# A four-layer graph network on one core: one-hot work split over two stages, 512 rows of zeros, deeper lags

## The reference

```python
h = jnp.maximum(_layernorm(x, axis=-1), 0.0)
x = x + _L0_gnn_ref(h, src, dst, edge_weight, ...)     # sum over edges into src of w * (h @ W)[dst], + bias
h = jnp.maximum(_layernorm(x, axis=-1), 0.0)
x = x + _L1_gnn_ref(h, edge_index, ...)                # attention: softmax over the edges into dst
h = jnp.maximum(_layernorm(x, axis=-1), 0.0)
x = x + _L2_gnn_ref(h, edge_index, ...)                # hypergraph: sum into dst, scale, sum back into src
h = jnp.maximum(_layernorm(x, axis=-1), 0.0)
x = x + _L3_gnn_ref(h, ..., src, dst, edge_attr_4, edge_attr_8, ...)  # tensor product, sum into dst
```

## Time and profile before

| | us |
|---|---|
| median of 3 runs (lowest to highest) | 3779.65 (3775.08 to 3782.87) |
| the profiled execution | 3784.34 |
| its span in the trace | 3782.5 |
| POOL busy (share of the span) | 2403.0 (64%) |
| DVE busy | 2003.5 (53%) |
| PE busy | 1933.2 (51%) |
| ACT busy | 920.8 (24%) |
| mean DMA rate | 115 GB/s |

### The profile page before, as it was taken

One profiled execution on the slowest core, in us unless ns is written; L12 is line 12 of the kernel. 1 busy time (PEld: TensorE's weight loads), 2 busy tenths in 40 slices (PEclk: granted clock), 3 DMA queues, 4 the chain that ended last, 5 costly groups with the idle time before them and its releaser, 6 DMA issues.

```text
span 3782.5 us, 39731 instructions
## 1 busy us (share of the span) xinstructions
PE 1933.2 (51%) x8526; PEld 1456.1 (38%) x8526; DVE 2003.5 (53%) x6412; ACT 920.8 (24%) x2412; POOL 2403.0 (64%) x2088
## 2 busy tenths in 40 slices
PE   0000037777668689889363233666666466664000
PEld 0000025555644367777253222443333365563000
DVE  6964325555999655554786555222222299995000
ACT  0000024443000144544133444222222222221000
POOL 0767777788880477775003564788888754448887
PEclk9999987777999755555576555555555578886555
DMA  2999623355650132332377998666666544445443
GB/s 82 297 298 333 209 59 87 84 66 68 97 66 0 33 80 78 78 80 66 94 230 134 114 124 121 138 120 130 119 124 126 115 144 145 140 143 96 37 36 34
DMA packets 449411, 437.32 MB, mean 116 GB/s; under 512 B 77855, under 2 KB 359493, under 8 KB 449027
## 3 DMA queue, kind: packets, MB, share of 16 engines
q0 software_dynamic: 128576, 119.75, 26.0%
q1 hardware_dynamic: 280262, 283.65, 23.8%
q10 hardware_dynamic: 40512, 33.32, 3.6%
HBM read 262.12 MB, written 174.41 MB: 115 GB/s over the span
## 4 chain that ended last, share of the span: by engine, by line
POOL 21%; DVE 9%; issue 8%; DMA 7%; PE 2%; ACT 2%; DVEq 1%; SPq 0%; ACTq 0%; POOLq 0%
POOL out_dram L654 15%; POOL work L640 5%; DVE work L1668 3%; DMA he<-work 3%; DMA work<-flags_clip 1%; DMA work<-gat_h 1%; DVE big L1998 1%; DVE work L1654 1%; DVE work L1963 1%; DVE work L1966 1%; PE bank L829 1%; ACT work L1175 1%; DVE work L1644 0%; DMA out_dram<-big,idx_add_d 0%; PE bank L954 0%
## 5 line engine op out<-in xcount | busy, mean ns | idle before, releaser
L1668 DVE TENSOR_TENSOR_SCAN work<-work,bank 128x512 f32<-128x512 f32 (+1 forms) x343 | 426.5, 1265 | 462.4 <-PE bank L829 220.4
L640 POOL DMA_INDIRECT work<-d,idx_run_d x196 | 189.6, 967 | 379.0 <-DVEq L286 264.6
L829 PE MATMUL bank<-ident,work 128*128 128x128 f32 x588 | 151.3, 407 | 456.1 <-ACT work L1175 238.6
L1175 ACT ACTIVATE work<-work 128x128 f32<-128x128 f32 x784 | 317.4, 481 | 257.8 <-DVE work L1663 244.0
L654 POOL DMA_INDIRECT out_dram<-work,idx_add_s x196 | 311.4, 1589 | 60.2 <-issue 59.1
L654 POOL DMA_INDIRECT out_dram<-big,idx_add_s x196 | 308.8, 1575 | 62.6 <-issue 53.7
L654 POOL DMA_INDIRECT out_dram<-big,idx_add_d x196 | 306.7, 1565 | 59.7 <-issue 55.2
L640 POOL DMA_INDIRECT work<-s,idx_e_d x196 | 203.4, 1038 | 209.9 <-DVE work L1963 160.0
L707 POOL DMA_INDIRECT big<-out_dram,idx_src_d x196 | 195.6, 998 | 200.7 <-DVEq L286 141.2
L829 PEld LDWEIGHTS bank<-ident,work 128*128 128x128 f32 x588 | 98.5, 204 | 508.3 <-ACT work L1175 176.8
L640 POOL DMA_INDIRECT work<-rec_d,idx_e_s x196 | 218.0, 1112 | 77.7 <-issue 58.2
(11 more groups left out here) (324 smaller groups left out, 5283.2 us busy)
## 6 DMA issues: line engine op xcount, KB each, us to landing
out_dram<-big SPq DMA_DIRECT2D x71, 726.0 KB, 8.2
big<-in_x_dram SPq DMA_DIRECT2D x71, 704.0 KB, 7.0
work<-flags_src SPq DMA_DIRECT2D x98, 256.0 KB, 3.8
work<-flags_dst SPq DMA_DIRECT2D x98, 256.0 KB, 3.7
edge_w<-work SPq DMA_DIRECT2D x49, 512.0 KB, 3.7
work<-edge_w ACTq DMA_DIRECT2D x49, 512.0 KB, 3.6
gat_h<-work SPq DMA_DIRECT2D x49, 256.0 KB, 2.5
work<-gat_h SPq DMA_DIRECT2D x49, 256.0 KB, 4.2
```

What stands on the lines that cost most here:

```text
L640: g_.indirect_dma_start(to, None, table_ap, bass.IndirectOffsetOnAxis(ap=f[:, at_:at_ + 1], axis=0)).then_inc(of_rows(name).of(G), 16)
L829: last = T.transpose(out[:, t * P:(t + 1) * P], of[:, t * P:(t + 1) * P], ident[:, :])
L1175: last = S_.activation(h[:, t * P:(t + 1) * P], v(t), ACT.Relu, bias=stat[:, 8 + t:9 + t], scale=stat[:, t:t + 1])
L1668: return V.tensor_tensor_scan(to, flag_r[G.place][rows, :], of, before if G.from_(1) else 0.0, ALU.mult, ALU.add)
```

## The change

There are five edits.

1. **GCN lags.** PE's `delta` and DVE's `chains` run two groups behind in place of one, ACT's `keep` three in place of two.
2. **Counting.** DVE only counts the equal keys. ACT takes for each tile the sum of signs of (key of the source - target key) by an activation with an accumulator (`n_sign`, new function `signs`), and `n_le` is worked out from both. `rank` uses eight banks in place of four.
3. **One list in place of two.** MAPS places `run_f` alone; the placing of `last_col`, which gives `sum_s`, moves into stage 7's loop: on DVE eight operations (four of 128x128 and four of 128x196) after `widen`, on PE four matmuls 196 columns wide after `net_out`. Both hand over through `HYPSUM["onehot"]` and `HYPSUM["placed"]`, with one buffer.
4. **512 rows of zeros.** `d1` ends with 512 rows of zeros (`GE`). An edge whose source is the target of no edge gets the row `EP + (partition | 128 * (tile mod 4))` in place of `EP`. SP stores 256 KB of zeros in stage 1 in place of 512 bytes.
5. **The last stage** alternates: `take(G)`, then `add(G - 6)`.

```diff
@@ stage 8, POOL
-            every_group(gathers("TP", s2_dram, [idx["sum_s"]], TP["taken"], D, in_r))
-            every_group(adds("TP", idx["add_d"], TP["kept"]))
+            take = gathers("TP", s2_dram, [idx["sum_s"]], TP["taken"], D, in_r)
+            add = adds("TP", idx["add_d"], TP["kept"])
+            late = 6
+            def body(G):
+                take(G)
+                if G.from_(late):
+                    add(group(G.g - late))
+            every_group(body)
+            for g in range(NG - late, NG):
+                add(group(g))
@@ stage 2, PE (DVE's chains and ACT's keep alike)
-                if G.from_(1):
-                    delta(G.before())
+                if G.from_(2):
+                    delta(G.before(2))
@@ stage 7, PE
+            def place(G):
+                pe.wait_ge(HYPSUM["onehot"], G.g + 1)
+                for t in range(GROUP):
+                    last = T.matmul(bank[7][:, 0:TILES], hot_s[:, t * P:(t + 1) * P], place_s[:, t * TILES:(t + 1) * TILES], ...)
+                last.then_inc(HYPSUM["placed"], 1)
             def body(G):
...
                 net_out(G)
+                place(G)
@@ stage 2, ACT
+            def signs(G):
+                if G.from_(1):
+                    act.wait_ge(MAPS["signed"], G.g)
+                act.wait_ge(MAPS["counted"], G.g + 1)
+                key, s = cols4(key_col["src"], G), cols4(n_sign, G)
+                for t in range(GROUP):
+                    last = S_.activation(junk[4 + t], bank[2 * G.place + t // 2][:, t % 2 * F:t % 2 * F + P], ACT.Sign,
+                                        bias=key[:, t:t + 1], scale=-1.0, accum_out=s[:, t:t + 1])
+                last.then_inc(MAPS["signed"], 1)
@@ stage 2, DVE
-                    for k, (c, op) in enumerate(((le, ALU.is_le), (eq, ALU.is_equal))):
-                        done(V.tensor_scalar(junk[2 * t + k], w, key[:, t:t + 1], None, op, ALU.add, accum_out=c[:, t:t + 1]))
+                    done(V.tensor_scalar(junk[t], w, key[:, t:t + 1], None, ALU.is_equal, ALU.add, accum_out=eq[:, t:t + 1]))
...
+            def onehot(G, hot, place, iota, row_c, col_c, of_c):
+                row, col, of = (cols4(c, G) for c in (row_c, col_c, of_c))
+                for t in range(GROUP):
+                    done(V.tensor_scalar(hot[:, t * P:(t + 1) * P], iota[:, 0:P], row[:, t:t + 1], None, ALU.is_equal))
+                    ins = V.tensor_scalar(place[:, t * TILES:(t + 1) * TILES], iota[:, 0:TILES], col[:, t:t + 1], of[:, t:t + 1],
+                                          ALU.is_equal, ALU.mult)
...
@@ stage 7, DVE
             def body(G):
                 chain(G, HYPSUM, "HYPSUM", [bank[G.slot]], uT_r, "delta")
                 widen(G)
+                if G.from_(1):
+                    dve.wait_ge(HYPSUM["placed"], G.g)
+                onehot(G, hot_s, place_s, iota_s, row_s, col_s, last_col).then_inc(HYPSUM["onehot"], 1)
```

More of the change, by code:

```diff
@@ L859, in body @@
                 turn(G)
-                if G.from_(1):
-                    delta(G.before())
+                if G.from_(2):
+                    delta(G.before(2))
             for_groups(pe, body)
+            delta(group(NG - 2))
             delta(group(NG - 1))
@@ L875, in rank @@
                 last.then_inc(MAPS["ranked"], 1)
+            pe.wait_ge(GCN["kept"], NG)
             for_groups(pe, rank)
+            pe.wait_ge(MAPS["signed"], NG)
             def place(G):
@@ L1019, in net_out @@
                 last.then_inc(HYPSUM["w"], 1)
+            def place(G):
+                pe.wait_ge(HYPSUM["onehot"], G.g + 1)
+                for t in range(GROUP):
+                    last = T.matmul(bank[7][:, 0:TILES], hot_s[:, t * P:(t + 1) * P], place_s[:, t * TILES:(t + 1) * TILES],
+                                    start=isinstance(G.g, int) and G.g == 0 and t == 0,
+                                    stop=isinstance(G.g, int) and G.g == NG - 1 and t == GROUP - 1)
+                last.then_inc(HYPSUM["placed"], 1)
             def body(G):
@@ L1199, in body @@
                 norm(G, GCN, lambda t: v_r[G.slot][:, t * P:(t + 1) * P], h_r[G.slot], GROUP, small[G.slot])
-                if G.from_(2):
-                    keep(G.before(2))
+                if G.from_(3):
+                    keep(G.before(3))
             for_groups(act, body)
+            keep(group(NG - 3))
             keep(group(NG - 2))
@@ L1709, in body @@
                 front(G)
-                if G.from_(1):
-                    chains(G.before())
+                if G.from_(2):
+                    chains(G.before(2))
                 scales(G, GCN, GROUP)
             for_groups(dve, body, order)
+            chains(group(NG - 2))
             chains(group(NG - 1))
@@ L1775, in onehots @@
                     dve.wait_ge(MAPS["placed"], G.g - 1)
-                row, col, of = cols4(row_f, G), cols4(col_f, G), [cols4(c, G) for c in (last_col, run_f)]
-                for t in range(GROUP):
-                    done(V.tensor_scalar(hot_r[G.slot][:, t * P:(t + 1) * P], iota_f[:, 0:P], row[:, t:t + 1], None, ALU.is_equal))
-                    for k in range(2):
-                        o = (2 * t + k) * TILES
-                        ins = V.tensor_scalar(place_r[G.slot][:, o:o + TILES], iota_f[:, 0:TILES], col[:, t:t + 1],
-                                              of[k][:, t:t + 1], ALU.is_equal, ALU.mult)
-                        if t < GROUP - 1 or k == 0:
-                            done(ins)
-                need(order.off)
-                ins.then_inc(MAPS["onehot"], 1)
+                onehot(G, hot_r[G.slot], place_r[G.slot], iota_f, row_f, col_f, run_f).then_inc(MAPS["onehot"], 1)
             for_groups(dve, onehots, order)
             dve.wait_ge(MAPS["placed"], NG)
-            link(V.tensor_copy(idx["sum_s"][:, :], bank[4][:, 0:TILES]))
-            link(V.tensor_copy(idx["run_d"][:, :], bank[4][:, TILES:2 * TILES]))
+            link(V.tensor_copy(idx["run_d"][:, :], bank[4][:, 0:TILES]))
             stage_end(dve, 2)
```

63 lines of the change are left out of this document (44 added, 19 removed).

## The result

The changed kernel takes **3477.84 us** (median of 4 runs, 3476.97 to 3484.99) against 3780.4 for the kernel before on the same chip (4 runs, 3775.08 to 3782.87): a ratio of **0.9206**, with a 95% interval of 0.919 to 0.9221. The forecast was 3504, the range 3435 to 3585. Two oddities among the runs stay unexplained: in one later set the kernel before itself took 4182.73 us (experiment 9), so numbers of that set are compared only with one another, and of the four executions of experiment 3 one took 7714.34 us and is left out of its ratio.

A forecast was written before the change was run, and what follows sets the result against it. Bounds: DVE in stage 2, slow zero-row reads in stage 6, POOL in stage 7, DVE then POOL in stage 8. From 3784.3 us, -137 - 63 + 64 - 140, less 4.7 for the median, gave 3504; range 3435 to 3585.

The forecast's parts named there:

- Stage 2: Shorter GCN lags, counting and one-hots let DVE finish before POOL's adds, so POOL sets the end: -137 us.
- The upper end for counting: Stage 2: four Signs on ACT plus as much again for reading four accumulators, 3.3 us a group, 162 us in all.
- no gain in GCN: Stage 2 if the deeper lag gained nothing: DVE ends at 1182, 53 us behind POOL, and 84 of 141 us are saved.
- Stage 6: 512 rows of zeros spread the gather's reads that hit one address; the stage takes 269 us: -63 us.
- The lower end: Stage 6: no gain, because the 512 rows of zeros lie side by side.
- Stage 7: Added placing makes one loop through PE, ACT and DVE, 13.7 us against POOL's 12.8: +64 us, ends 0 and +131.
- Rival B: Stage 7: the clock stays at 1.2 GHz and the loop is 15.1 us: +67, 3571 us; chance 0.25.
- rival C: Stage 7: the loop stays under POOL's 12.8 us: -64, 3440 us; chance 0.15.
- Stage 8: Alternating gathers and adds keeps POOL working without a wait, 645 us against 785.3: -140 us.
- The rule against it: Skill's claim that GpSimd cannot write DMA descriptors during VectorE two-port operations, so overlaps would cost POOL the DVE operation's time.
- E: Stages 2 and 7: POOL gives way to DVE's one-hots: +176 together, 3680 us; chance 0.05.
- Rival F: Stage 8: adds stretch beside DVE's work, 3.0 us each losing the whole gain; +363, 3867 us; chance 0.03.

The follow-up runs named there:

- experiment 9: Earlier set, kernel before at 4182.73 us; changed kernel with GCN lag of one 3988.98, eight zero rows 3866.32, 64 zero rows 3862.22, both counts on DVE 3892.79 us.
- experiment 3: Changed kernel with every edge whose source is no target reading the first of the 512 rows of zeros: 3550.81 us, ratio 0.9387.
- experiment 1: Changed kernel with both lists placed in stage 2 again and nothing placed in stage 7: 3425.59 us, ratio 0.9055.
- experiment 5: Changed kernel with GCN's lags put back (PE's delta and DVE's chains one group behind): 3520.13 us, ratio 0.9302.
- experiment 6: Changed kernel with both counts on DVE again and no signs on ACT: 3480.65 us, ratio 0.92.
- experiment 7: Changed kernel with eight rows of zeros in use in place of 512: 3480.76 us, ratio 0.9205.
- experiment 2: Changed kernel with PE's `place` in stage 7 moved to right after `delta`, one group later: 3427.7 us, ratio 0.9068.
- experiment 4: Changed kernel with stage 8 doing all gathers, then all adds, again: 3637.55 us, ratio 0.9613.

## Why the prediction came out right

The 26 us between 3504 and 3478 are 31 us too little gain in the stages (276 forecast, 307 measured), less 5 for the difference between profiled execution and median, taken as 4.7 us off and in the changed kernel close to nothing.

- **Stage 2** (-137 forecast, -136.6 measured). The end is POOL's, as said. The terms behind it: GCN 5.45 us a group for 6.0, counting 2.4 for 2.3, one-hots 2.2 for 2.5; DVE ends at 1040 where 1075 was forecast. That POOL is the end made these misses free. The upper end for counting, 3.3 us, took reading an accumulator to be as long as the Sign itself and to stand behind it; it is 0.20 us and lies inside the Signs, which come every 0.34 us, so ACT needs 1.5 us a group (the "1.9 at least" was too high as well) and waits 53.1 / 49 = 1.1 for DVE, whose 2.4 set the time. The 504 ns for a one-hot beside adds were read as the price of each; they hold for those that an add hits (experiment 1), which is part of why the 2.5 was too high.
- **Which edit it was.** The prediction credited 137 us to three edits together. Undone one at a time they give back 39, 0 and 0 us of stage 2 (experiments 5, 6 and 1), because the other two leave slack. Edit 1 is worth the most, 133 us of DVE's line. Edits 2 and 3 are worth 44 and 78 there, and neither is needed if the other stays; with both undone the line would be 122 us longer against 92 of slack, so some 30 us would show. That is an estimate from experiments 1, 5 and 6, and no run tests it. The prediction had said that with no gain in GCN 84 of the 141 us would be saved, with DVE 53 us behind POOL; measured, it is 41.
- **Stage 6** (-63, -68.3). The cause is shown by experiments 3 and 7: 0.57 us a packet from one row, 0.137 from eight, 0.145 from 512. The lower end, no gain because the rows lie side by side, is refuted already by eight rows. The stage's length under POOL's work was put 5 us too high.
- **Stage 7** (+64, +52). The mechanism is shown by experiments 1 and 2: one loop through PE, ACT and DVE in place of POOL's 12.8 us. The slow loop was put at 15.1 and is 15.05; the fast one saves 2.7 where "2.4 us at most" was forecast. The mis-sized term is the average, 1.4 of 15.1, which is 1.6: 48 x 0.22 = 11 us. That it came so close is in part luck: no row said how often the clock would rise, and the "bit over half" of the groups happened to fit a loop in which it rises in every second one and in the first few. Rival B had the slow loop right for those groups in which the clock doesn't rise; rival C would have needed the fast loop, 12.35, in nearly every group, and they alternate with slow ones.
- **Stage 8** (-140, -152). Alternation is shown by experiment 4. Gathers cost 0.975 us for 1.03, adds 1.602 for 1.58: 250 + 373 = 623 for 631, and the ends 10 us for 14. (The better end of this term, 3.13 us a pair, comes to -158 by its own sum and not to -155.) The gathers' mean was taken from a stretch in which they stood beside DVE's heaviest work.
- **The rule against it.** Adds beside the one-hots of stage 2 take 1594 ns on average (56 of them, 930 to 1036), those after DVE's end 1554 (47, 1042 to 1128): 40 ns, 2.6%; in experiment 1, 1564 ns, only 10. The Trainium skill (SBUF — State Buffer, section "SBUF: two separate sides") would have POOL's descriptor writing wait for the two-port operation; if adds took turns with DVE's 107 us of one-hots, stage 2 would have ended about that much later. The measurement decides against E: such a loss isn't there. What is there is smaller and falls on the other side, 0.2 to 0.3 us of one DVE operation in each add; whether the one-hots are two-port operations, no row here shows. Rival F, adds at 3.0 us in stage 8, isn't either.

## What to carry to other kernels

Before work is moved off an engine, ask at what time its line is due: here one-hots worth 78 us left a place where they were hidden. Their new place was between two steps of PE's in-order queue, where PE had to wait for the answer to its own last step, and that cost 52 us; one group later, behind a step that waits for nothing of the kind, the same work was free. Undo edits one at a time, since several that hide one another look like a joint gain, and add up what each takes from the engine that is hidden: what two of them are worth together can't be read from the total time that either gives back. Where a gather reads one row thousands of times, a handful of copies of that row, by some bits of the position, is enough.

## What the hardware showed

- **One address read over and over:** 0.57 us for a packet of 2 KB when 80% of the rows read are one row, 0.137 when they are eight neighbouring rows (4 KB in all). DMA engines then count as busy to 0.93 while 116 GB/s move; a high busy share at a low rate is the sign.
- **The clock from group to group:** in stage 7 the same instructions ran in 12.35 and 15.05 us next to each other, the clock risen by the end of the same 4.62 us of work in the one and not in the other, in turns over 42 groups. A mean of such a loop is a mix of two lengths, and more work on PE (447 us in place of 393) came with a higher clock, 0.63 for 0.50.
- **POOL beside DVE:** each accumulating indirect DMA of POOL lengthens one DVE operation by 0.2 to 0.3 us (experiment 1: 94 operations for 97 adds, 0.57 to 0.66 us in place of 0.37) and leaves the rest as they are. Means hide this: 409 ns for the 128x196 one-hot that takes 376 alone, or 505 and 374 for two equal ones. The add itself grows by 10 to 40 ns.
- **Reading ACT's accumulator** is a record of its own, 0.20 us, but the next activation doesn't wait for its end: Signs of 0.37 us start 0.34 us apart with the readings between them.
- **A kernel's sensitivity to its surroundings:** in one set of runs all kernels were 11 to 13% slower, most of it in stages 2, 3 to 5 and 6. The cause stays open. Edits worth 0 and 39 us at other times were worth 31 and 127 us there.
